# Half Toeplitz matrices and a fused scan step in an S4D-plus-MoE kernel

## What is computed

```python
x_in = x @ in_W.T + in_b
u = jnp.swapaxes(x_in, 1, 2)                  # (2 sequences, 128 channels, 2048 steps)
K = jnp.exp(dtA[:, :, None] * jnp.arange(Lseq))   # 32 complex states a channel
k = 2.0 * jnp.einsum('hn,hnl->hl', Ceff, K).real  # one impulse response a channel
y = jnp.fft.irfft(rfft(u, n) * rfft(k, n), n)[..., :Lseq] + u * D_skip[:, None]
y = jax.nn.gelu(y, approximate=False)
```

## Time and profile before

| what | value |
|---|---|
| median of 3 runs | 339.66 us |
| profiled execution, its own time | 338.3 us |
| profiled execution, its span from first to last instruction | 336.5 us |
| mean granted TensorE clock, share of full | 0.928 |
| TensorE busy (share of the span) | 273.8 us (81%) |
| VectorE busy | 224.1 us (67%) |
| ScalarE busy | 168.2 us (50%) |
| GpSimd busy | 175.0 us (52%) |

### The profile page before, as it was taken

The page is one execution under the profiler, slowest core; times in us unless marked ns, Lnnn a source line. Parts: engine busy times, 40 slices in busy tenths (PEclk is TensorE's granted clock), DMA queues, the critical chain, the costliest instruction groups (busy, mean ns, idle before and its releaser), DMA issues.

```text
span 336.5 us, 9262 instructions
## 1 busy us (share of the span) xinstructions
PE 273.8 (81%) x2856; PEld 243.7 (72%) x2856; DVE 224.1 (67%) x851; ACT 168.2 (50%) x340; POOL 175.0 (52%) x231
## 2 busy tenths in 40 slices
PE   1892755775898887888796997799999999999970
PEld 0892645654775564766595997799999999999920
DVE  6999998999522888688888441135556555555673
ACT  1569353787754686577747322244444444444400
POOL 2589100000370017777777774165777776777740
PEclk9999696995999797999959799799999999999995
DMA  5790027979970001111111351322423334333769
GB/s 142 223 421 26 0 83 207 266 216 290 332 191 0 2 1 56 50 53 50 57 49 55 99 121 47 88 71 69 112 73 105 96 85 111 93 92 94 272 215 290
DMA packets 54290, 41.29 MB, mean 123 GB/s; under 512 B 6215, under 2 KB 50140, under 8 KB 53744
## 3 DMA queue, kind: packets, MB, share of 16 engines
q1 hardware_dynamic: 47264, 31.20, 32.6%
q0 software_dynamic: 4544, 8.47, 7.6%
q10 hardware_dynamic: 2448, 1.20, 1.3%
HBM read 28.74 MB, written 13.02 MB: 124 GB/s over the span
## 4 chain that ended last, share of the span: by engine, by line
DVE 26%; issue 22%; PE 20%; POOL 11%; DMA 9%; SPq 4%; ACT 3%; DVEq 2%; POOLq 1%; ACTq 0%
POOL y_dram L621 8%; SPq L418 3%; POOL xs_dram L615 3%; DVE u L727 3%; PE bank L1448 2%; DMA area<-kp_dram 2%; PE bank L1664 2%; DVE v L367 2%; PE bank L1675 2%; DVE stats L682 2%; PE bank L1488 2%; PE bank L1496 2%; DMA kp_dram<-xnT 2%; DVE area L716 2%; DMA area<-y_dram 1%
## 5 line engine op out<-in xcount | busy, mean ns | idle before, releaser
L621 POOL DMA_INDIRECT y_dram<-u x78 | 78.1, 1001 | 39.3 <-issue 23.5
L615 POOL DMA_INDIRECT xs_dram<-area x64 | 62.9, 983 | 42.8 <-issue 41.3
L1000 DVE COPY v<-v 128x512 f32 x84 | 39.7, 473 | 29.1 <-issue 28.9
L1664 PE MATMUL bank<-xn,v 128*128 128x128 f32 x320 | 42.8, 277 | 0.5 <-ACT xn L1299 0.5
L1675 PE MATMUL bank<-v,xn 128*128 128x128 f32 x312 | 42.2, 279 | 0.3 <-ACT xn L1304 0.3
L1664 PEld LDWEIGHTS bank<-xn,v 128*128 128x128 f32 x320 | 39.2, 193 | 0.8 <-issue 0.7
L1675 PEld LDWEIGHTS bank<-v,xn 128*128 128x128 f32 x312 | 38.8, 195 | 0.7 <-ACT xn L1304 0.7
L1304 ACT ACTIVATE xn<-bank 128x512 f32<-128x512 f32 x40 | 23.9, 597 | 22.7 <-PE bank L1664 21.9
L1299 ACT COPY xn<-bank 128x256 f32<-128x256 f32 x41 | 15.2, 370 | 28.4 <-PE bank L1655 28.4
L1018 DVE COPY u<-area 128x2 uint32<-128x2 uint32 x39 | 6.9, 178 | 27.0 <-PE bank L1675 26.4
L1212 ACT ACTIVATE area<-x_sb,shift,tbuf 128x128 f32<-128x128 f32 x32 | 13.2, 482 | 18.4 <-DVE shift L930 18.4
(11 more groups left out here) (307 smaller groups left out, 640.2 us busy)
## 6 DMA issues: line engine op xcount, KB each, us to landing
area<-kp_dram SPq DMA_DIRECT2D x12, 512.0 KB, 7.1
area<-xs_dram SPq DMA_DIRECT2D x78, 65.0 KB, 1.8
x_sb<-in_L_attn_x SPq DMA_DIRECT2D x4, 512.0 KB, 7.6
area<-ab_dram SPq DMA_DIRECT2D x2, 1024.0 KB, 5.6
xn<-ab_dram SPq DMA_DIRECT2D x2, 1024.0 KB, 10.3
xn<-kp_dram SPq DMA_DIRECT2D x4, 512.0 KB, 6.6
area<-y_dram SPq DMA_DIRECT2D x4, 512.0 KB, 6.6
area<-y_dram SPq DMA_DIRECT2D x8, 256.0 KB, 5.1
```

The costliest lines, as they stand in the source:

```text
L615: pool.indirect_dma_start(out=xs_dram.ap(), out_offset=bass.IndirectOffsetOnAxis(ap=pos[:, k, i:i + 1], axis=0), in_=hx[:, i, k, :], in_of ...
L621: pool.indirect_dma_start(out=y_dram.ap(), out_offset=bass.IndirectOffsetOnAxis(ap=ybi[:, z:z + 1].bitcast(U32), axis=0), in_=yb[:, z, :], ...
L1000: v.tensor_copy(wc[:, z % STEP], v1_flat.rearrange("p (w m) -> p w m", w=2)[:, :, bass.ds(r, HID)]).then_inc(wc_ready, 1)
L1664: last = mm(bank[2 + p % 2][:, HID * j + P * c:HID * j + P * c + P], wc[:, (2 * p + j) % STEP, 1, P * c:P * c + P], xsT[:, p % 3, P * j:P ...
```

## The change

Three parts.

**Toeplitz matrices.** The matrix is lower triangular and Toeplitz, so its last 64 input steps against output steps 64 to 127 are the same 64 x 64 block as its first 64 input steps against output steps 0 to 63. Only the 64 rows of the first 64 input steps are loaded, 128 elements each. Half of a group's channels have them on partitions 0 to 63, the other half on 64 to 127 (`side`). A channel is then two matmuls with a contraction over 64 partitions: `early` inputs times 128 columns, and `late` inputs times the first 64 columns, added to output columns 64 to 127.

**u with swapped halves.** One of the two operands lies on the wrong half of the partitions, so two new DMAs copy `u` with its partition halves swapped for the channels that need it (`u_other`, 64 partitions x 2048 elements each), queued on SyncE between the loads of groups 0 and 1.

**Scan step.** The step factors stand in `rot`, written once by four small copies on VectorE behind a new wait for `mag_ready`. A step is one product of 256 columns (both parts of the old state times their two factors), written over the two places before the raw state of chunk j, and one `tensor_reduce` over three neighbouring columns. `st` is shifted by one column; results go to `states_at`, in the first 2048 columns of `v1`, behind a new wait `v2_ps` of 4. The loads of `w2_sb` write there too, so SyncE now waits for `sbd_act` and `sbd_dve` before them.

```diff
+        raw_states, shifted = [st[:, i:i + 2 * NX * NT].rearrange("p (r x b j) -> p r x b j", r=2, x=NX, b=B) for i in range(2)]
+        states_at = v1_flat[:, 0:2 * NX * NT].rearrange("p (r x b j) -> p r x b j", r=2, x=NX, b=B)
...
+        u_other = xn_flat[:, 0:2048].rearrange("p (g h c) -> p g h c", g=NG, c=NT)
+        rot = xn_flat[:, 2048:2304].rearrange("p (k r m) -> p k r m", k=2, r=2)
...
-            for g in range(NG):
-                if g == 0:
-                    sp.wait_ge(v1_dve, 4)
-                elif g == 1:
-                    sp.wait_ge(mag_ready, NG)
-                    sp.wait_ge(abb_used, NG)
-                else:
-                    sp.wait_ge(v1_dve, 2 * NG)
+            def load_toeplitz(g):
+                sp.wait_ge(v1_dve, 4 if g < 3 else 2 * NG)
                 sp.wait_ge(kp_out[g], 16)
                 for b in range(4):
-                    src = bass.AP(kp_dram, (g * P + 32 * b) * 256, [[1, P], [256, 8], [1, P]])
-                    sp.dma_start(hank[g][:, 8 * b:8 * b + 8, :], src).then_inc(hank_in[g], 16)
+                    side = b // 2
+                    src = bass.AP(kp_dram, (g * P + 32 * b) * 256 + 64, [[1, 64], [256, 8], [1, P]])
+                    sp.dma_start(hank[g][64 * side:64 * side + 64, 8 * (b % 2):8 * (b % 2) + 8, :], src).then_inc(hank_in[g], 16)
+
+            load_toeplitz(0)
+            sp.wait_ge(abb_used, 3)
+            sp.wait_ge(u_ready, 8)
+            for side in range(2):
+                src = u_flat.rearrange("p (g s h c) -> p g s h c", g=NG, s=2, c=NT)[64 - 64 * side:128 - 64 * side, :, side]
+                sp.dma_start(u_other[64 * side:64 * side + 64], src).then_inc(hank_in[0], 16)
+            for g in range(1, NG):
+                load_toeplitz(g)
...
+            sp.wait_ge(sbd_act, 1)
+            sp.wait_ge(sbd_dve, 1)
             for c in range(HC):
...
             dve.wait_ge(lw_act, 1)
+            dve.wait_ge(mag_ready, NG)
...
+            for c, r, i in ((0, 0, 0), (0, 1, 4), (1, 0, 3), (1, 1, 0)):
+                last = v.tensor_copy(rot[:, c, r].rearrange("p (x b) -> p x b", b=B),
+                                     lw[:, i].unsqueeze(2).broadcast_to([P, NX, B]))
+            link(last)
...
+            dve.wait_ge(v2_ps, 4)
+            after_, prev_ = [t_.rearrange("p r x b j -> p r (x b) j") for t_ in (states_at, raw_states)]
+            three = st[:, 0:2 * NX * NT].rearrange("p (r m j) -> p r m j", r=2, j=NC)
+            link(v.tensor_copy(after_[:, :, :, 0], prev_[:, :, :, 1]))
             for j in range(1, NC - 1):
-                v.tensor_tensor(m1, lr_b, sv[:, :, :, :, j - 1], ALU.mult).then_inc(dve_step, 1)
-                v.tensor_tensor(m2, li_b, sv[:, ::-1, :, :, j - 1], ALU.mult).then_inc(dve_step, 1)
-                dve.wait_ge(dve_step, steps[0] + 1)
-                steps[0] += 2
-                link(v.tensor_tensor(sv[:, :, :, :, j], sv[:, :, :, :, j], m1, ALU.add))
-                link(v.tensor_tensor(sv[:, :, :, :, j], sv[:, :, :, :, j], m2, ALU.add))
+                was = after_[:, :, :, j - 1].unsqueeze(2).broadcast_to([P, 2, 2, 2 * NX])
+                link(v.tensor_tensor(three[:, :, :, j - 1:j + 1].rearrange("p r m k -> p k r m"), rot[:], was, ALU.mult))
+                link(v.tensor_reduce(after_[:, :, :, j], three[:, :, :, j - 1:j + 2], AX.X, ALU.add))
...
-                pe.wait_ge(hank_in[g], 64)
+                pe.wait_ge(hank_in[g], 64 if g else 96)
                 for q in range(HG):
-                    h = HG * g + q
+                    h, side, i = HG * g + q, q // 16, q % 16
                     k, x_ = h % 4, h // 4
-                    last = mm(bank[x_ // 4][32 * k:32 * k + 32, P * (x_ % 4):P * (x_ % 4) + P], u[:, h, :], hank[g][:, q, :],
-                              start=(x_ % 4 == 0), stop=False, skip_group_check=True)
+                    rows = slice(64 * side, 64 * side + 64)
+                    early, late = (u_other[rows, g, i], u[rows, h, :]) if side == 0 else (u[rows, h, :], u_other[rows, g, i])
+                    out_ = bank[x_ // 4][32 * k:32 * k + 32, P * (x_ % 4):P * (x_ % 4) + P]
+                    mm(out_, early, hank[g][rows, i, :], start=(x_ % 4 == 0), stop=False, skip_group_check=True)
+                    last = mm(out_[:, 64:P], late, hank[g][rows, i, 0:64], start=False, stop=False, skip_group_check=True)
```

More of the change, by code:

```diff
@@ L111, in build_kernel @@
         s_bd = sb("s_bd", [P, NPAIR, 2, NT])
-        st = sb("st", [P, 2, NX, NT])
+        st = sb("st", [P, 2 * NX * NT + 1])
+        raw_states, shifted = [st[:, i:i + 2 * NX * NT].rearrange("p (r x b j) -> p r x b j", r=2, x=NX, b=B) for i in range(2)]
         v1_flat = v1[:].rearrange("p h r n -> p (h r n)")
-        hank = [h_.rearrange("p (h t) -> p h t", h=HG)
-                for h_ in (area[:, 8192:12288], xn_flat, area[:, 0:4096], area[:, 4096:8192])]
+        states_at = v1_flat[:, 0:2 * NX * NT].rearrange("p (r x b j) -> p r x b j", r=2, x=NX, b=B)
+        hank = [h_.rearrange("p (h t) -> p h t", t=P)
+                for h_ in (area[:, 8192:10240], area[:, 10240:12288], area[:, 4096:6144], area[:, 6144:8192])]
+        u_other = xn_flat[:, 0:2048].rearrange("p (g h c) -> p g h c", g=NG, c=NT)
+        rot = xn_flat[:, 2048:2304].rearrange("p (k r m) -> p k r m", k=2, r=2)
         yq = area[:, 0:4096]
@@ L207, in build_kernel @@
         rw = sb("rw", [P, E])
-        rmsn = st[0:EA, 1, 24:28, :].rearrange("p x c -> p (x c)")
+        rmsn = st[0:EA, 1792:1792 + P]
         rmsT = sb("rmsT", [P, EA])
@@ L373, in state_copy @@
             dst = s_bd[64 * e + 32 * r:64 * e + 32 * r + 32, m::2, e, :].rearrange("p x (b c) -> p x b c", b=B)
-            src = st[32 * k:32 * k + 32, r].rearrange("p x (b c) -> p x b c", b=B)
-            return dst[:, :, :, lo + 1:hi + 1], src[:, :, :, lo:hi]
+            return dst[:, :, :, lo + 1:hi + 1], states_at[32 * k:32 * k + 32, r, :, :, lo:hi]
         def y_tiles(i):
@@ L772, in weigh_states @@
                 shape = [P, 2, 8, NT]
+                s_ = st[:, 1:].rearrange("p (r x c) -> p r x c", r=2, c=NT)[:, :, x_]
                 own = bank[g][:].rearrange("p (r x c) -> p r x c", r=2, x=8)
                 cross = rnd[:, 512 * (g % 2):512 * (g % 2) + 512].rearrange("p (r x c) -> p r x c", r=2, x=8)
-                v.tensor_tensor(st[:, :, x_], lw[:, 1:3, x_].unsqueeze(3).broadcast_to(shape), own, ALU.mult)
+                v.tensor_tensor(s_, lw[:, 1:3, x_].unsqueeze(3).broadcast_to(shape), own, ALU.mult)
                 link(v.tensor_tensor(cross, lw[:, 5, x_].unsqueeze(1).unsqueeze(3).broadcast_to(shape), own[:, ::-1], ALU.mult))
-                v.tensor_tensor(st[:, :, x_], st[:, :, x_], cross, ALU.add).then_inc(st_dve, 1)
+                v.tensor_tensor(s_, s_, cross, ALU.add).then_inc(st_dve, 1)
             for g in range(NG):
```

## The result

| | kernel before | kernel changed |
|---|---|---|
| median, us | 338.88 (20 runs, 336.38 to 341.59) | 342.22 (20 runs, 339.48 to 346.71) |
| ratio, 95% interval | | 1.0095 (1.0067 to 1.0123) |
| profiled execution, own time and span | 338.3, 336.5 | 341.9, 340.0 |
| convolution starts, reading of the states starts | 68.28, 88.30 | 68.56, 89.87 |
| scan's side ready (ScalarE's copies end) | 87.42 | 86.23 |

The change costs 3.2 us (2.3 to 4.2), where -0.5 was forecast. It is slower by more than the 0.5% that counts as a difference, and inside the range of 336.6 to 342.8.

What follows compares the result with a forecast made beforehand. The stage was taken to end when both TensorE's convolution (87.8 us, held by late program parts) and the scan with its copies (86.9) are done. 87.8 against 88.3 gave -0.5: 339.66 - 0.5 = 339.2 us, range 336.6 to 342.8.

Steps and rivals of the forecast that it cites:

- the period of a piece: TensorE's convolution: time between arrivals of successive 16 KB parts of its program, each about 127 record pairs; about 5.3 us.
- the forecast's 76.2, 81.5, 86.8 and 87.8: Convolution on TensorE: predicted arrivals in us of three successive program parts, then the convolution's end.
- The sum: Reading of the states starts at max(87.8, 86.9) + 0 = 87.8 us, before 88.3: -0.5 us, put on the median.
- the effect of w1: SyncE's queue: w1's loads go out some 5 us sooner, ahead of w2's new wait; cost nothing.
- The mechanism: TensorE's program arrives in parts of about 127 record pairs, the next requested when one is begun; 2.3 us idle at first.
- The loads leave the path: Toeplitz loads, 5 MB instead of 8: group 2 lands by 72 to 75 us, group 3 by 79, before TensorE needs them.
- A group's cost of 3.05 us: Convolution on TensorE: 1.95 us plus 64 late records at 17 ns each, bounds 15 and 30 ns.
- Scan step of 1.34 us: VectorE's scan: product 0.61 us, sum 0.65 and two gaps of 0.04, between 1.14 and 1.54; before 1.41.
- Copies into `rot`, `u_other`, w2's wait: Small copies on VectorE (0.6 us, hidden), two extra issues and a later w2 load on SyncE; each to cost nothing.
- the slower side: Rival: clock falls while TensorE waits for instructions, +2.9 us, 342.6; with slow program parts (+1.9) or dear scan, chance 0.22.
- Blocking of early and late: Rival: a channel's two matmuls block each other in the array, convolution ends near 99.9 us, +11.6 us; chance 0.04.
- The scan's side binds: Rival: scan and state copies end last, centre 86.5 us, -1.8 us, 337.9; chance 0.30, including both sides fast.

Runs made afterwards that it cites:

- w1_later: The changed kernel with w1's two loads moved behind SyncE's waits for the copies of the states; ratio to the kernel before 1.0015 (0.9977 to 1.0053).
- split_columns: The kernel before with each convolution matmul cut into two of 64 columns, loads and scan unchanged; ratio 1.0039 (0.9973 to 1.0104), from 4 of 12 executions.
- conv_only: The changed kernel with the old scan step of four instructions and w2 loaded without the new wait; ratio to the kernel before 1.015 (1.009 to 1.0209).
- no_unused: The changed kernel without the unused matmuls ahead of groups 2 and 3; ratio to the kernel before 1.0152 (1.0083 to 1.0221).
- after_again: The changed kernel run once more, unaltered, for a second profile; ratio to the kernel before 1.011 (1.0027 to 1.0192).
- no_late: The changed kernel without the late matmuls, so part of the convolution is left out; ratio to the kernel before 0.9995 (0.9956 to 1.0034).
- scan_w1: The kernel before with the new scan step and w1's loads behind the waits for the copies; ratio 1.0001 (0.9962 to 1.004).
- mixed: The kernel before with the new scan and half matrices, two matmuls a channel, for groups 2 and 3 only; ratio 1.0073 (1.0034 to 1.0112).

## Why the prediction was wrong

**The step that failed is the period of a piece.** I took 5.3 us, the mean of 5.9, 6.1, 5.7, 4.6 and 4.4, two of which were only upper bounds. The changed kernel's were 5.1, 7.0, 5.9 and 7.6. The two short ones, nearest to the stage, came from 62 to 71 us, where the windows of before show a DMA share of 0.69 (64 to 68.5) and 0.79 (68.5 to 73.6); in the changed kernel it was 1.11 to 1.23 from 73.6 to 83.7. A mean over both was not the price of a piece there. That the fuller DMA makes the difference is shown by w1_later for the pieces behind 80 us. From the forecast's 76.2, 81.5, 86.8 and 87.8 the execution shows 75.81, 82.83, 88.75 and 89.87: -0.4 on the first piece, +1.7 and +0.6 on the two periods, +0.1 on the last records, together the 2.07 us by which the join missed 87.8 (the four round to 2.0). The +1.7 is the piece's. TensorE had its work of that piece done 6.46 us after it began (75.81 to 82.27) where 4.6 was forecast, since the clock was at the 1.2 GHz level from 77.2 to 80.7; but it then waited another 0.56 us, so the slower work only filled a wait that was there.

This step accounts for 2.1 of the 3.7 us between forecast (-0.5) and result (+3.2). The sum also put nothing behind the join: "+ 0", and the difference on the median as it is. The fourth late piece, inside the reading, stood against that with 0.45 us. The rest is under what stays open.

**I also let the effect of w1 pass.** "w1 goes out ahead, some 5 us sooner than before" stands in the prediction, at a cost of nothing, because its reader is far away. The issue came 5.6 us sooner. What it met was not a reader but the next packet of the program. With 512 records the ratio is 1.0095 and with the edit 1.0015; with 256 it is 1 by definition and with the edit 0.9981. The two gains differ by 0.6%, and the four intervals leave some 0.7% of doubt on that (an estimate), so it is the packets' starts and the gaps, more than the ratios, that show it.

Point by point:

* *The mechanism* (program in pieces of 127 or 128 record pairs, the next asked for when one is begun, gaps inside the convolution) is shown for the pieces and their size: by the gaps' places in the changed kernel, split_columns, conv_only, no_unused and after_again, and by the two packets more. That the next is asked for when one is begun fits the packets of 0.4 to 0.7 us; the one near 44 us leaves it open. The Trainium skill, "Advanced Engine Details and Errata", section ISA Cache, names 128 KB for TensorE, by which this side would end at 84.5. The trace disagrees (gaps every 128 records); its two lines of 16 KB agree.
* *The loads leave the path:* right. No wait of L1454 for a DMA. The rate was 202 to 210 GB/s, not the 230 taken, and in no_late group 3 landed at 80.9, not by 79.
* *A group's cost of 3.05 us:* too dear. Group 0 takes 68.56 to 71.19, 2.63 us at full clock, from its first record to the next group's. Measured in the same way, before's takes 1.78 (68.28 to 70.06; the 1.95 that I used has the last record's tail in it). So a late record costs (2.63 - 1.78) / 64 = 13.3 ns, a little below my lower bound of 15. Harmless, since the pieces decided.
* *Scan step of 1.34 us:* 1.27 measured (66.06 to 83.85 over 14), product 0.62 and sum 0.58 against 0.61 and 0.65. The side was ready at 86.23, not 86.9. It gains 1.2 us against before and none of it counts.
* *Copies into `rot`, `u_other`, w2's wait:* no loss seen. The copies take 0.50 us at 50.35 and `states(2)` goes on at 56.27, as before.
* *The rivals:* the slower side, at a chance of 0.22, held, but by its slow pieces and not by its clock. Pieces at 6.1 us were to give a join 1.9 us behind before's, at 90.2; the three periods of the convolution were 6.0 on average, and the join came 1.6 behind, at 89.87. The clock did fall, to 0.50 for 3.4 us, in spite of the unused matmuls that I set against it. Yet the work of that piece, 6.46 us, stayed below its measured period of 7.0, so the clock did not decide; no_unused shows what it costs when it stays low for 17 us. Blocking of early and late is refuted by the 13.3 ns. The scan's side binds in w1_later and no_late within 0.9 us.

**What stays open.** The join explains 1.6 us in one profile and 1.0 in the other, the fourth gap, inside the reading, 0.45 more. That is carried on unchanged: at the end of the reading the two are 2.03 and 1.42 us behind before, at the 49th of the 64 writes to `xs_dram`, near 188 us, 2.05 and 1.41. The next stage then varies by itself. Between the last write to `xs_dram` and the first to `y_dram` GpSimd stands idle for 10.18 us in before, 10.97 in the changed kernel and 8.85 in after_again:

```profile
217.34 1.25 POOL L621 DMA_INDIRECT y_dram<-u  x1 [10.18 <-DVE u L1019]
220.40 1.24 POOL L630 DMA_INDIRECT y_dram<-u  x1 [10.97 <-DVE u L1031]
217.47 1.24 POOL L630 DMA_INDIRECT y_dram<-u  x1 [8.85 <-DVE u L1031]
```

So 1.4 to 2.0 us of the loss are placed, and the medians differ by 3.3; one profile a kernel can't tell whether the rest is the change's.

Nor does a join earlier than that of before come out as time. In w1_later it is 1.7 us ahead of before's, in a profile that is the fastest of its 12 executions, and the ratio is 1.0015. Its lead is 2.35 us at the first write to `xs_dram` and 0.73 at the 17th; in between the mean granted clock is 0.85, in before 0.92. scan_w1 loses its lead in the same stretch, also at 0.85. No run shows why the clock is lower there.

## What to carry to other kernels

TensorE's program is itself a stream of loads, and it shares the DMA engines with yours. When a change doubles the matmuls of a stretch, count its records against 128 a piece and set the period from a stretch in which the DMA is as full; then look at which large loads, even ones nobody waits for, run in the same microseconds, and move these first. Halving the bytes paid less than half here, where the halves lie on 64 partitions and a load is half as large: the engines stayed as full and moved over a quarter less.

## What the runs showed that I had not expected

* The instruction packet's wait: 0.4 to 0.7 us with the DMA idle behind the Toeplitz loads, 2.3 to 5.0 us beside loads in the changed kernel, 3.2 to 3.9 near 44 us with the DMA all but idle; then 2.2 to 3.2 us to the first record wherever TensorE waited for it, over the fourteen profiles. The packet itself takes about 1.2 us (2.5% of 16 engines in the 3 us of w1_later shown above).
* Loads of 256 KB onto 64 partitions moved 202 to 215 GB/s at a DMA share of 1.16 to 1.23, those of 512 KB onto 128 partitions 285 to 301 at 1.15 to 1.19. So 5 MB instead of 8 freed the queue less than their bytes say. No run separates the partitions from the size of a load.
* The clock is not the wait's alone: in mixed, 1.40 us without a matmul and busy stretches on either side were followed by 13.6 us at 0.50, in w1_later 2.07 us by 0.60 for 4 us and then 0.97.
* No kernel was told apart as faster than the one before. The changed kernel with w1 later is level with it (0.9977 to 1.0053), and so is the new scan step with whole matrices, with w1 later (0.9962 to 1.004).
